# Cross-attention and FFN block on one core: normalised tiles turned in 32x32 blocks by VectorE by way of DRAM, output projection over four PSUM banks

## The reference, cut to what matters

```python
x = x + xattn(layernorm(x), ctx, ctx, Wq, Wk, Wv, Wo)   # x: 16 x 112 tokens x 1024, float32
x = x + ffn(layernorm(x), w1, w1_scale, w3, w3_scale, w2, w2_scale)
# xattn: 32 query heads, 8 key/value heads of 32; its last step is out @ Wo (1024 x 1024)
# ffn: g = n @ w1.T; u = n @ w3.T; y = (silu(g) * u) @ w2.T, 1024 -> 3584 -> 1024
```

## Time and profile before

| | us |
|---|---|
| median of 3 runs | 2532.99 (2530.29 to 2537.29) |
| the profiled execution | 2538.41 |
| its span in the profile | 2536.6 |
| `mixing`, its first matmul of tile 1 to the first instruction of `ffn` | 879.35 to 1041.17 |
| PE / DVE / ACT / POOL busy over the span | 96% / 67% / 39% / 22% |

### The profile page before, as it was taken

One profiled execution on the slowest core, in us unless ns is written; L12 is line 12 of the kernel. 1 busy time (PEld: TensorE's weight loads), 2 busy tenths in 40 slices (PEclk: granted clock), 3 DMA queues, 4 the chain that ended last, 5 costly groups with the idle time before them and its releaser, 6 DMA issues.

```text
span 2536.6 us, 35412 instructions
## 1 busy us (share of the span) xinstructions
PE 2427.8 (96%) x12682; PEld 2071.4 (82%) x12682; DVE 1698.4 (67%) x2639; ACT 979.2 (39%) x1673; POOL 559.2 (22%) x305
## 2 busy tenths in 40 slices
PE   7998999999999799599999998999999999999999
PEld 6997878878875488489999987988988978888887
DVE  6425777777776344688888888888888874445442
ACT  3212445445444321354444444444433443233231
POOL 1000344454455300001111111322333320000000
PEclk9998999999998799799999999999999999999999
DMA  7535555555545335456555564565776687555652
GB/s 226 173 92 138 140 139 139 144 134 142 143 110 131 95 127 170 119 183 184 159 176 156 158 179 134 158 174 190 208 209 176 172 287 234 172 174 160 183 161 86
DMA packets 369146, 408.04 MB, mean 161 GB/s; under 512 B 125824, under 2 KB 324096, under 8 KB 359152
## 3 DMA queue, kind: packets, MB, share of 16 engines
q1 hardware_dynamic: 369008, 406.22, 56.1%
HBM read 252.99 MB, written 152.70 MB: 160 GB/s over the span
## 4 chain that ended last, share of the span: by engine, by line
PE 44%; DVE 8%; DMA 3%; issue 2%; SPq 1%; ACT 1%; DVEq 0%; ACTq 0%
PE bank L84 15%; PE bank L85 14%; PE bank L86 14%; DMA stash<-weight_scratch 3%; DVE g_WL L90 2%; DVE g_XL L90 1%; DVE g_su L1699 1%; DVE xT L1655 1%; SPq L1431 1%; DVE stash L1667 1%; DVE stash L1666 1%; DVE stash L1669 1%; ACT stash L1548 0%; ACT g_WH L1558 0%; DVE stash L1643 0%
## 5 line engine op out<-in xcount | busy, mean ns | idle before, releaser
L84 PE MATMUL bank<-g_XH,g_WH 128*128 128x448 f32 (+1 forms) x2254 | 848.0, 376 | 51.8 <-DVE g_su L1699 24.2
L85 PE MATMUL bank<-g_XL,g_WH 128*128 128x448 f32 (+1 forms) x2254 | 845.0, 375 | 0.0
L86 PE MATMUL bank<-g_XH,g_WL 128*128 128x448 f32 (+1 forms) x2254 | 844.8, 375 | 0.0
L84 PEld LDWEIGHTS bank<-g_XH,g_WH 128*128 128x128 f32 x2254 | 425.2, 189 | 115.8 <-DVE g_WL L90 52.8
L86 PEld LDWEIGHTS bank<-g_XH,g_WL 128*128 128x128 f32 x2254 | 425.2, 189 | 54.1
L85 PEld LDWEIGHTS bank<-g_XL,g_WH 128*128 128x128 f32 x2254 | 425.4, 189 | 53.5
L1558 ACT ACTIVATE g_WH<-stash 128x512 fp32r<-128x512 f32 x392 | 241.7, 627 | 427.6 <-PE bank L86 247.0
L90 DVE TENSOR_TENSOR g_WL<-stash,g_WH 128x512 fp32r<-128x512 f32 (+1 forms) x417 | 336.0, 809 | 77.4 <-ACT g_WH L1558 49.4
L696 DVE TENSOR_REDUCE a_nm<-bank 112x1 f32<-112x375 f32 x512 | 264.9, 531 | 116.9 <-PE bank L831 113.3
L800 ACT ACTIVATE a_pr<-bank 125x448 f32<-125x448 f32 x384 | 204.8, 545 | 208.2 <-PE bank L907 153.7
L649 POOL TENSOR_TENSOR a_prsum<-a_pr 125x1792 f32<-125x1792 f32 x32 | 129.3, 4039 | 365.3 <-ACT a_pr L800 365.3
(11 more groups left out here) (132 smaller groups left out, 3592.8 us busy)
## 6 DMA issues: line engine op xcount, KB each, us to landing
stash<-in_L_ffn_w SPq DMA_DIRECT2D x168, 256.0 KB, 5.1
weight_scratch<-stash SPq DMA_DIRECT2D x28, 1024.0 KB, 7.7
stash<-weight_scratch SPq DMA_DIRECT2D x28, 1024.0 KB, 7.4
h_scratch<-g_Sh SPq DMA_DIRECT2D x112, 224.0 KB, 3.9
down_scratch<-xT SPq DMA_DIRECT2D x98, 256.0 KB, 3.1
stash<-in_ctx SPq DMA_DIRECT2D x48, 500.0 KB
stash<-h_scratch SPq DMA_DIRECT2D x25, 896.0 KB, 6.7
a_qst<-q_scratch SPq DMA_DIRECT2D x96, 224.0 KB, 4.7
```

The source lines that it names most:

```text
L84: pe.matmul(acc, lh, rh, start=first, stop=False, skip_group_check=onto)
L85: pe.matmul(acc, lh, rl, start=False, stop=False, skip_group_check=onto)
L86: return pe.matmul(acc, ll, rh, start=False, stop=last, skip_group_check=onto)
```

## The change

The eight TensorE transposes of a tile and ScalarE's copies out of PSUM are gone. Instead the normalised tile is written plainly, stored to a new DRAM tensor `norm_scratch`, loaded again by four DMAs that place its 32x32 blocks (`load_turn`) into a new buffer `xr`, and turned within the blocks by two VectorE transposes (`turn_tile`). The four banks that this frees are used by the products in turn, so that products(t) needs the additions of tile t-2 and not t-1. VectorE turns tile t-2 after it has normalised tile t. The last tile is turned inside `ffn`. For semaphores, the loads of y in the down projection share two counters for each half, with a wait between.

```diff
@@ load_turn and turn_tile, new
+        def load_turn(sp, dst, t, loaded):
+            cols = n_scr[t * P:(t + 1) * P, :].rearrange("(c i) (q n) -> q i c n", i=BL, q=Q4)
+            for q in range(Q4):
+                sp.dma_start(dst[q * BL:(q + 1) * BL, :, :], cols[q]).then_inc(loaded, 16)
+        def turn_tile(src, dst, turned):
+            src = src.rearrange("p c (b j) -> p b c j", j=BL)
+            dst = dst.rearrange("p b (c j) -> p b c j", j=BL)
+            nc.vector.transpose(dst[:, 0:KH], src[:, 0:KH])
+            return nc.vector.transpose(dst[:, KH:KT], src[:, KH:KT]).then_inc(turned, 1)
@@ mixing, sync
                         def store_xT(t):
-                            sp.wait_ge(t_out, 2 * t + 2)
+                            sp.wait_ge(turned, t + 1)
...
+                        def load_xr(t):
+                            sp.wait_ge(xn_stored[t % 2], 16 * (t // 2 + 1))
+                            wait(sp, turned, t - 1)
+                            load_turn(sp, xr[:, t % 2, :, :], t, xr_loaded[t % 2])
...
                             sp.wait_ge(y_done, 2 * t + 2)
                             sp.dma_start(y_scr[t * P:(t + 1) * P, :], yb[:, t % 2, :]
                                          ).then_inc(res_stored[t % 2], 16)
-                            if t > MT:
-                                store_xT(t - 1)
-                        store_xT(NT_TOK - 1)
+                            sp.wait_ge(xn_done, t + 1)
+                            sp.dma_start(n_scr[t * P:(t + 1) * P, :], xn[:, t % 2, :]
+                                         ).then_inc(xn_stored[t % 2], 16)
+                            if t:
+                                load_xr(t - 1)
+                            if t > MT + 1:
+                                store_xT(t - 2)
+                        store_xT(NT_TOK - 2)
@@ mixing, vector
+                        def turn(t):
+                            dve.wait_ge(xr_loaded[t % 2], 64 * (t // 2 + 1))
...
                             residual_norm(t)
+                            if t >= 2:
+                                turn(t - 2)
+                        turn(NT_TOK - 2)
@@ mixing, tensor
-                                pe.wait_ge(y_done, 2 * t + n - 1)
+                                wait(pe, y_done, 2 * (t - 2) + n + 1)
...
                             products(t)
-                            transposes(t - 1)
-                        transposes(NT_TOK - 1)
@@ ffn, sync, and vector
+                        load_turn(sp, last_in, NT_TOK - 1, last_loaded)
...
                             if mi == 2:
+                                sp.wait_ge(last_turned, 1)
+                                sp.dma_start(x_scr[:, :, HALF - P:HALF], last_out
+                                             ).then_inc(last_stored, 16)
...
+                                sp.wait_ge(last_stored, 16)
                                 sp.dma_start(xT[:, :, :], x_scr).then_inc(x_loaded_, 16)
...
+                                if mi == 0 and i == 1:
+                                    dve.wait_ge(last_loaded, 64)
+                                    turn_tile(last_in, last_out, last_turned)
```

More of the change, by code:

```diff
@@ L952, in mixing @@
                 rstd_done, xn_done = s_("rstd"), s_("xn")
-                t_done, t_out = s_("t_done"), s_("t_out")
-                o_bank, t_bank = bank[0:2], bank[2:4]
+                turned = s_("turned")
+                xr_loaded = [s_("xr_loaded0"), s_("xr_loaded1")]
                 with nc.Block() as block:
@@ L1055, in residual_norm @@
                             dve.wait_ge(rstd_done, t + 1)
[L1056 to L1062 removed]
+                            wait(dve, xn_stored[slot], 16 * (t // 2))
+                            nc.vector.tensor_scalar(xn[:, slot, :], yb[:, slot, :], aggr[:, 0:1],
+                                                    rstd[:], ALU.subtract, ALU.mult
+                                                    ).then_inc(xn_done, 1)
+                        def turn(t):
+                            dve.wait_ge(xr_loaded[t % 2], 64 * (t // 2 + 1))
+                            if t >= MT:
+                                wait(dve, xT_stored[t % 2], 16 * ((t - MT) // 2))
+                            turn_tile(xr[:, t % 2, :, :], xT[:, :, t * P:(t + 1) * P] if t < MT
+                                      else xs[:, t % 2, :, :], turned)
                         split_attention(0)
@@ L1092, in products @@
                                 last.then_inc(o_done, 1)
-                        def transposes(t):
-                            pe.wait_ge(xn_done, t + 1)
-                            for kh in range(2):
-                                wait(pe, t_out, 2 * t + kh - 1)
-                                for k in range(KH):
-                                    last = pe.transpose(t_bank[kh][:, k * P:(k + 1) * P],
-                                                        xn[:, t % 2, KH * kh + k, :], ident[:])
-                                last.then_inc(t_done, 1)
                         pe.wait_ge(a_lo, 1)
@@ L1195, in ffn @@
                            + [su[:, :, :].rearrange("p k n -> p (k n)")[:, k * FB:(k + 1) * FB] for k in range(2)])
-                d_y_loaded = [[sem(f"d_y_loaded{r}{t}") for t in range(MT)] for r in range(2)]
+                d_y_loaded = [[sem(f"d_y_loaded{r}{k}") for k in range(2)] for r in range(2)]
                 d_a_loaded = [sem("d_a_loaded0"), sem("d_a_loaded1")]
@@ L1245, in load_a, with y_count @@
                                  ).then_inc(d_a_loaded[n % 2], 16)
+                def y_count(r, t):
+                    return sum(32 * len(rows(r, u)) for u in range(t % 2, t + 1, 2))
                 def load_y(sp, r, t):
+                    if t >= 2:
+                        sp.wait_ge(d_y_loaded[r][t % 2], y_count(r, t - 2))
                     for at, n, tok in rows(r, t):
@@ L1336, in out_tile @@
                         if i == 0:
-                            nc.vector.wait_ge(d_y_loaded[0][t], 32 * len(rows(0, t)))
+                            nc.vector.wait_ge(d_y_loaded[0][t % 2], y_count(0, t))
                             nc.vector.tensor_copy(v, acc).then_inc(v_done, 1)
```

48 lines of the change are left out of this document (21 added, 27 removed).

## The result

The median went from 2532.64 us (2530.29 to 2537.29; a fourth run has joined the three of the table above) to **2590.69 us** (2586.52 to 2597.05, four runs): a ratio of 1.0229, 95% interval 1.0203 to 1.0255, 58 us slower. The profiled execution took 2586.52 us, the shortest of the four.

A forecast was written before the change was run, and what follows sets the result against it. TensorE was taken to bound the loop before, and SyncE's queue with the attention load after the change. The median of 2533.0 us plus 39 us in `mixing` and 0 in `ffn` gave 2572 us, range 2556 to 2592.

The forecast's parts named there:

- The loop closes over the attention load; TensorE stops being the bound.: Loop of `mixing`: attention load queues behind normalisation, store and four loads, so TensorE waits 3 to 4.5 us, twelve times.
- A tile of 14.5 us, then 15.6.: Loop of `mixing`: 14.5 us from low part to low part instead of 11.78, and 15.6 in the second half.
- The four loads: SyncE's queue in each tile of `mixing`: issuing four 128 KB loads to 32 partitions takes 1.7 us.
- Tile 2's low part 891.6: Early in `mixing`: tile 2's low part, done at 889.63 before, comes 2.0 us later, at 891.6.
- The end 14.7 us: End of `mixing`: 14.7 us from the last product to the start of `ffn`, before 9.3 us.
- The last product 11.15: Last tile of `mixing`: the last product takes 11.15 us and ends at 1065.6.
- `mixing` +39: Whole of `mixing`: 39 us longer, with `ffn` beginning at 1080.3 instead of 1041.2.
- `ffn` 0, at most 4: `ffn`: its added loads, turn and wait for the last tile's store are covered, 0 us, up to 4 for the range.
- The sum.: Whole kernel: median before of 2533.0 plus 39 us gives 2572 us.
- Staying hidden or nearly cancelling: Two rivals in the loop: loads stay hidden, 2527 us, 4%; gain and loss cancel within 0.3%, 4%.
- The queue backing up: Rival in the loop's DMA queue: attention load lands 1.5 us later, tile 16 to 17 us, 2588 us, 10%.
- The clock: Rival on TensorE: its clock falls in each wait; 2 us once, or 2604 us if whole products run low, 4%.

The follow-up runs named there:

- e3: Kernel before, TensorE transposes kept, plus SyncE's wait, store of the normalised tile and four loads that nobody reads: 2576.5 us, ratio 1.0185.
- e1: Kernel after, with the attention load of tile t+2 moved right behind y's store, ahead of the wait: 2533.9 us, ratio 1.0010.
- e4: Kernel after, with the last turned tile's store in `ffn` issued one weight tile earlier: 2578.9 us, ratio 1.0187.
- e8: Kernel after, with one plain 128-partition load of the same bytes in place of the four for tiles 0 to 12: 2570.0 and 2570.9 us.
- e7: Kernel before, with only its products put over four banks in turn: 2531.8 us, ratio 0.9997.
- e12: e5 with VectorE's turn put back behind the normalisation except in the last tile: 2538.7 us, ratio 1.0019.
- e2: Kernel before, with only SyncE's wait for the normalised tile added, no transfer: 2537.7 us, ratio 1.0017.
- e5: e9 with the four loads moved ahead of the wait for y and the turn ahead of the normalisation: 2534.8 us, ratio 1.0004.
- e9: Kernel after, with the attention load ahead of the wait and the last tile's store one weight tile earlier: 2528.2 us, ratio 0.9976.
- e6: Kernel after, with the four loads and then the attention load ahead of the wait for the normalised tile and its store: 2559.4 us, ratio 1.0096.
- e11: Kernel after, with the attention load behind the normalised tile's wait and store but ahead of the four loads: 2557.0 us, ratio 1.0092.
- e10: e9 with tile 12's four loads and tile 11's turn moved early in the last tile alone: 2528.8 us, ratio 0.9974.

## Why the prediction was right, and where its size was off

The forecast was 2572 us, the range 2556 to 2592, the direction slower; measured 2590.7, inside the range at its dear end, 19 us above the forecast. Step by step:

- *The loop closes over the attention load; TensorE stops being the bound.* Shown: TensorE waited twelve times for the low part (3.3 us in the mean, 5.7 at the most, forecast 3 to 4.5); e3 gives the loss without touching TensorE, e1 takes it away without touching the work.
- *A tile of 14.5 us, then 15.6.* Tiles 3 to 10 took (1011.57 - 890.86) / 8 = 15.09, tiles 11 to 13 (1061.16 - 1011.57) / 3 = 16.53. By term: low part to normalised tile 4.56, as forecast; its store 0.37 (0.38); high and low part 2.31, as forecast. **The four loads** took 2.24 to 2.33 us to issue in tiles 3 to 10, not 1.7: I priced them by L151, whose median came from a stage with an emptier queue, and the 2.81 us of the earlier trace rows was the nearer row. Issue to ScalarE took 5.0 to 6.3 us, 5.5 in the mean as forecast, in tiles 3 to 10, and 5.9 to 6.7, 6.3 in the mean and not 6.0, in tiles 11 to 13. So the issue was mis-sized throughout and the landing in the second part only. A tile came out 0.6 and 0.9 us longer than forecast: 8 x 0.6 + 3 x 0.9 = 7.5 of the 8 us by which `mixing` exceeded the forecast.
- *Tile 2's low part 891.6*, 13.1 us behind the first addition; it was 13.7 behind it.
- *The end 14.7 us*: 14.45. The last product 11.15: 11.2.
- *`mixing` +39*: +47.0.
- *`ffn` 0, at most 4*: this step failed. I took 4.0 us for the landing of the last tile's store from the earlier trace rows and let the 8.6 us in which the queue was idle cover it. But the store stands right behind a weight load and a weight store of 1 MB each, so it landed after 9.9 us; h's stores and the weight load then bunched, the load took 6.43 us to issue instead of 4.00, and TensorE waited 5.3 us for its data and then ran at the lower clock for a while. By e4 it is worth 7.5 us. The row of a landing in an idle queue was used for one in a full queue.
- *The sum.* 47.0 + 7.5 = 54.5 us, against 58 in the medians. Of the missing 3.5 us no run shows the source; the kernel after's profiled run is the shortest of its four, and e4, with the same `mixing` code, took 3.2 us more in it. In the two profiles the spans differ by 48.1 only, since the profile of before stayed on the slower of `ffn`'s two rates (last section).
- *Rivals.* Staying hidden or nearly cancelling: excluded. The queue backing up: a part of it came true, the landing at most 0.8 us longer than taken and not 1.5. The clock: it fell, but not in every wait. Six of the twelve products took 11.2 us and the other six 12.8 to 13.4 (from 905.51 to 918.28, for one, the granted clock was 0.87). Even so TensorE was done at least 1.2 us before the next low part came, so it cost nothing in the loop, as reasoned. The forecast put its price in the last product, where there is nothing to hide behind: here that one took 11.2 us at 1.00, which is luck, since in e8 it took 12.7 at 0.87. (The dear form of that rival, 2604, comes out nearer to 2601: 11 x 17.4 in place of 162.8 us adds 29.) The page "TensorE: Matmul & The Clock Gate" of the Trainium skill, section "HAM oscillation — how this bites in real kernels", describes such a fall in every round of a loop that waits for DMAs. The trace agrees for half of the rounds, and shows that it is free there, as the load sets the round.
- *The transposes 0.9 us a tile, 11.7 in all*: 0.84 a tile in e1, 10.9 in all. *The banks nothing*: e7, nothing. What of the gain a kernel can keep is e1's 157.0 in `mixing`, 5.7 us, since the longer end takes 5.3 of the 10.9 back.

## What to carry to other kernels

An engine that issues DMAs in order is a resource of its own: before a wait is put into its queue, list what stands behind the wait and how much slack that has. Here a load with 2.4 us to spare was put 5 us back, which cost 47 us, and one tile's loads moved ahead again gave them all back. Price issue and landing by rows with the same traffic ahead in the queue, not by the median of a calm stage; and a move that makes a load early is worth something only if what the load itself waits for is early too.

## What the runs showed of the hardware that I had not expected

- A store's landing depends on what is ahead of it in the queue. The store of the normalised tile, always the same 0.5 MB, landed 2.8 to 3.2 us behind its issue in the kernel after (tiles 1 to 13), 5.5 to 7.2 in e1, where an attention load and a load of x stand just ahead (tiles 1 to 11), and 6.8 to 8.7 in e12, where y's store and four loads stand ahead of those too. The last turned tile took 9.9 us behind a weight load and a weight store of 1 MB each, 8.5 in e4; the same size took 4.0 in the earlier trace rows.
- Four loads to 32 partitions each cost 2.2 to 2.5 us of issue in the rounds shown, up to 3.1 in e1 (1.73 to 1.75 in a calm stretch); one load of the same bytes to 128 partitions cost 0.43.
- The first half of `ffn` runs at one of two rates, both at a granted clock of 1.00: four weight tiles behind the fifth take 69.44 us in the profiles of before, e2, e5, e9 and e12 and 68.09 us in the others, which is some 7 us over `ffn`. From start to start, a matmul of 448 columns costs 206.7 or 202.7 ns. By stretch, the kernel before and the kernel after at the same work (instructions in brackets):

```profile
1250.00:1350.00 100.00, 100.00 (x485) 90.82 (x484) 85.55 (x128) 48.03 (x82) 14.89 (x10) 1.00 0.59 173
```

```profile
1300.00:1400.00 100.00, 100.00 (x496) 92.68 (x495) 87.34 (x130) 49.03 (x84) 16.99 (x12) 1.00 0.60 175
```

TensorE is busy in all of both, with 485 matmuls in the one and 496 in the other. In all fourteen profiles the rate in this half stays as it is from one wait of TensorE to the next, and changes only across a wait. The kernel after ran at 206.7 ns up to the wait of 5.3 us and at 202.7 behind it, e12 at 202.7 up to a wait of 0.6 us in the same place and at 206.7 behind it. The five profiles with the late store (after, e1, e6, e8, e11) all have the faster rate behind their wait, too few to tell whether the longer wait brings it. The cause stays open; it does not go with the code of this stretch, since e9 and e10 differ in the last tile of `mixing` alone and show one rate each. The groups of runs of e9 and e10 fit it: the profile at the slower rate is of a run of the upper group (2533.4 us), the one at the faster of a run of the lower (2523.9). A difference of a few us in `ffn` between two single profiles is therefore no finding.
